# Token scatters of a two-layer gated cross-attention and mixture-of-experts kernel: four in a row per batch, or one by one over two units and over the expert blocks

## The reference, cut to what matters

```python
x = x + tanh(g_xattn[0]) * attention0(layernorm(x), ctx, ctx, mask)
x = x + tanh(g_ffn[0]) * experts0(layernorm(x))     # silu(x@gate[e]) * (x@up[e]) @ down[e], hidden width 688
x = x + tanh(g_xattn[1]) * attention1(layernorm(x), ctx, ctx)
x = x + tanh(g_ffn[1]) * experts1(layernorm(x))     # relu(x@w1[e])**2 @ w2[e], hidden width 256
```

## Time and profile before

| what | value |
|---|---|
| median of three runs | 711.34 us |
| the profiled execution, its span | 741.8 us |
| its own time | the profile gives the span; no other time of that execution is shown |
| PE (TensorE) busy | 659.3 us, 89% |
| DVE (VectorE) busy | 407.1 us, 55% |
| ACT (ScalarE) busy | 271.6 us, 37% |
| POOL (GpSimd) busy | 221.4 us, 30% |
| TensorE clock granted, mean | 0.972 |
| layer 0 units, blocks | 0 to 160 us, 160 to 464 us |
| layer 1 units, blocks | 464 to 612 us, 612 to 722 us |
| last combination and output | 722 to 742 us |

### The profile page before, as it was taken

One profiled execution on the slowest core, in us unless ns is written; L12 is line 12 of the kernel. 1 busy time (PEld: TensorE's weight loads), 2 busy tenths in 40 slices (PEclk: granted clock), 3 DMA queues, 4 the chain that ended last, 5 costly groups with the idle time before them and its releaser, 6 DMA issues.

```text
span 741.8 us, 17801 instructions
## 1 busy us (share of the span) xinstructions
PE 659.3 (89%) x6008; PEld 481.6 (65%) x6008; DVE 407.1 (55%) x1375; ACT 271.6 (37%) x531; POOL 221.4 (30%) x405
## 2 busy tenths in 40 slices
PE   8889887789999999999999999989888888789960
PEld 6657666557777777777775555667666656578730
DVE  3888778774444323332332223688888775554416
ACT  4555555542211111121111112467666432244430
POOL 5123434433231111111111111124655344544430
PEclk9999999999999999999999999999999999899995
DMA  9243434552124111101311100601111132443329
GB/s 231 68 136 124 142 123 169 183 178 67 44 101 120 38 36 29 36 30 36 82 33 41 30 15 18 232 30 31 59 60 59 59 101 86 144 122 115 108 72 339
DMA packets 49960, 69.14 MB, mean 93 GB/s; under 512 B 7751, under 2 KB 37319, under 8 KB 49875
## 3 DMA queue, kind: packets, MB, share of 16 engines
q1 hardware_dynamic: 40620, 49.00, 21.8%
q0 software_dynamic: 6528, 17.90, 6.8%
q10 hardware_dynamic: 2727, 1.11, 0.6%
HBM read 45.76 MB, written 22.23 MB: 92 GB/s over the span
## 4 chain that ended last, share of the span: by engine, by line
PE 70%; DVE 14%; issue 5%; another core or an unknown queue 5%; DMA 2%; ACT 2%; POOL 1%; SPq 0%; ACTq 0%; DVEq 0%; POOLq 0%
PE ps L1764 26%; PE ps L1810 16%; DVE m_rows L981 4%; PE ps L1550 4%; PE ps L1787 3%; PE ps L1488 3%; PE ps L1542 3%; PE ps L1505 2%; PE ps L1588 2%; PE ps L1564 2%; DVE x_sb L965 2%; DVE ctx_q L998 1%; PE ps L1516 1%; DVE share L1003 1%
## 5 line engine op out<-in xcount | busy, mean ns | idle before, releaser
L1764 PE MATMUL ps<-w_all,share 128*128 (+1 forms) x720 | 213.2, 443 | 8.2 <-DVE share L1125 5.8
L1764 PEld LDWEIGHTS ps<-w_all,share 128*128 128x128 f32 (+1 forms) x720 | 125.2, 180 | 73.6 <-issue 13.9
L629 POOL DMA_INDIRECT ys_dram<-share,dest_i x72 | 69.1, 960 | 297.1 <-DVE share L1346 247.5
L1810 PE MATMUL ps<-w_all,share 112*128 (+3 forms) x576 | 139.1, 385 | 5.0 <-ACT share L864 4.3
L1810 PEld LDWEIGHTS ps<-w_all,share 112*128 112x128 f32 (+3 forms) x576 | 98.2, 180 | 24.8 <-issue 8.6
L1405 DVE TENSOR_TENSOR share<-share,ps 128x344 f32<-128x344 f32 x72 | 37.0, 514 | 122.1 <-PE ps L1764 54.1
L981 DVE TENSOR_REDUCE m_rows<-ps 128x8 f32<-128x960 f32 x64 | 70.6, 1143 | 14.4 <-PE ps L1505 9.9
L845 ACT COPY share<-ps 128x512 f32<-128x512 f32 x36 | 21.1, 585 | 141.2 <-PE ps L1787 141.2
L600 POOL DMA_INDIRECT xs_dram<-xn,slot_now x64 | 63.6, 994 | 30.0 <-issue 14.0
L840 ACT ACTIVATE share<-ps 128x344 f32<-128x344 f32 x72 | 32.9, 457 | 96.8 <-PE ps L1764 71.4
L577 POOL TENSOR_SCALAR nm<-mv 128x1 f32<-128x1 f32 (+1 forms) x48 | 11.6, 242 | 157.5 <-DVE mv L1021 120.4
(11 more groups left out here) (235 smaller groups left out, 1102.8 us busy)
## 6 DMA issues: line engine op xcount, KB each, us to landing
w_all<-ys_dram SPq DMA_DIRECT2D x16, 512.0 KB, 7.3
share<-xs_dram SPq DMA_DIRECT2D x56, 129.0 KB
w_all<-gate SPq DMA_DIRECT2D x8, 688.0 KB
w_all<-up SPq DMA_DIRECT2D x8, 688.0 KB
w_all<-down SPq DMA_DIRECT2D x8, 560.0 KB
w_all<-w SPq DMA_DIRECT2D x16, 256.0 KB
share<-xs_dram SPq DMA_DIRECT2D x32, 64.5 KB
out<-x_sb SPq DMA_DIRECT2D x8, 256.0 KB, 5.6
```

Of the source, the lines that this page charges most:

```text
L629: g.indirect_dma_start(ys_dram, bass.IndirectOffsetOnAxis(ap=dest_i[:, u:u + 1], axis=0), y_sb[:, u, :], None).then_inc(D_y[u], 16)
L1764: i = t.matmul(ps[0:r, bank, 0:w], xgT[:, k, 0:r], w_all[:, bass.ds(off + (k * UPW[l] + col - EW[l]), w)], start=(k == 0), stop=(k == KT - 1))
L1810: i = t.matmul(ps[0:n, 6, 0:D], h[:, 0:n], w_all[0:r, bass.ds(off + (KT * UPW[l] + c * D - EW[l]), D)], start=(c == 0), stop=(c == KD[l] - 1))
```

## The change

The scatters get a semaphore for each tile. In an even unit of batch b >= 3 GpSimd now does: the token numbers, scatter (0, 0) of batch b-3, in layer 1 the second addition of batch b+2, a wait for this unit's shifted scores, scatter (0, 1), ln2_rstd of the unit before, ln1_rstd of batch b+2. In the odd unit: scatter (1, 0), in layer 1 the first addition of batch b+3, the same wait, scatter (1, 1), ln2_rstd. After the units the four scatters of batch 5 are placed behind waits for the first up products of blocks 0, 1 and 2 (`up_done`; b_up counts four steps for each of layer 0's blocks and one for each of layer 1's), with the last ln2_rstd and the pad's tile of zeros after the second; then come store 0 and the scatters of batches 6 and 7, each behind block 2 to 9's up products and each ahead of a store. ln2_apply waits for the tile that it overwrites alone; slots and SP wait for both tiles. Nothing is computed differently.

```diff
--- before.py
+++ after.py
@@ -239,7 +239,7 @@
         L_last = sem("last_expert_loaded")
         L_xg = [sem(f"block_loaded{u}") for u in range(U3)]
         D_y = [sem(f"block_stored{u}") for u in range(U3)]
-        D_sc = [sem(f"tokens_scattered{b}") for b in range(NB)]
+        D_sc = [[sem(f"tile{t}_scattered{b}") for t in range(2)] for b in range(NB)]
         D_pad = sem("pads_scattered")
         D_gl = [sem(f"results_loaded{b}") for b in range(NB)]
         D_out = [sem(f"out_stored{i}") for i in range(2)]
@@ -353,9 +353,9 @@
 
             return j // U3 + BLOCKS // U3 * l
 
-        def scattered(B):
-
-            return D_sc[B % NB], 64 * (B // NB + 1)
+        def scattered(B, t):
+
+            return D_sc[B % NB][t], 32 * (B // NB + 1)
 
         UP = [[(0, 0, 344), (1, HID[0], 344), (2, 344, 344), (3, HID[0] + 344, 344)], [(0, 0, HID[1])]]
         REST = (HID[0] - P) // (KD[0] - 1)
@@ -452,7 +452,8 @@
 
                 sp.wait_ge(d_l1, 14 * (l + 1))
                 for b in range(EARLY):
-                    sp.wait_ge(*scattered(NB * l + b))
+                    for t in range(2):
+                        sp.wait_ge(*scattered(NB * l + b, t))
                 sp.wait_ge(p_q, 2 * NB * (l + 1))
                 for j in range(2):
                     load_block(j)
@@ -598,7 +600,7 @@
             def scatter_rows(B, t, k):
                 s = (NU * (B // NB) + 2 * (B % NB)) % 6
                 g.indirect_dma_start(xs_dram, bass.IndirectOffsetOnAxis(ap=slot_now[:, B % 2, t, k:k + 1], axis=0),
-                                     xn2[:, s + t, :], None).then_inc(scattered(B)[0], 16)
+                                     xn2[:, s + t, :], None).then_inc(scattered(B, t)[0], 16)
 
             def token_numbers(B):
                 b = B % NB
@@ -607,12 +609,6 @@
                 g.tensor_copy(xn2[:, s:s + 2, D], tokid[:, 2 * b:2 * b + 2]).then_inc(g_id, 1)
                 g.wait_ge(g_id, B + 1)
                 g.wait_ge(d_slot, B + 1)
-
-            def scatter(B):
-                token_numbers(B)
-                for t in range(2):
-                    for k in range(TOPK):
-                        scatter_rows(B, t, k)
 
             def add_results(b, k):
 
@@ -643,39 +639,58 @@
                     B, G = NB * l + b, NU * l + u
                     if even:
                         if b >= 3:
-                            scatter(B - 3)
-                    elif b + 2 < NB:
-                        ln1_rstd(B + 2)
-                    if u > 0:
+                            token_numbers(B - 3)
+                            scatter_rows(B - 3, 0, 0)
+                        if l == 1 and BY_V <= b + 2 < NB:
+                            add_results(b + 2, 1)
+                        if b >= 3:
+                            g.wait_ge(p_e, G + 1)
+                            scatter_rows(B - 3, 0, 1)
+                        if u > 0:
+                            ln2_rstd(G - 1)
+                        if b + 2 < NB:
+                            ln1_rstd(B + 2)
+                    else:
+                        if b >= 3:
+                            scatter_rows(B - 3, 1, 0)
+                        if l == 1 and BY_V <= b + 3 < NB:
+                            add_results(b + 3, 0)
+                        if b >= 3:
+                            g.wait_ge(p_e, G + 1)
+                            scatter_rows(B - 3, 1, 1)
                         ln2_rstd(G - 1)
-                    if l == 1 and not even and BY_V <= b + 3 < NB:
-                        add_results(b + 3, 0)
-                        add_results(b + 3, 1)
-                scatter(NB * l + NB - 3)
+                B5, B6, B7 = (NB * l + NB - n for n in (3, 2, 1))
+
+                def up_done(j, n):
+
+                    g.wait_ge(b_up, 4 * j + n if l == 0 else 4 * BLOCKS + j + 1)
+
+                token_numbers(B5)
+                scatter_rows(B5, 0, 0)
+                up_done(0, 2)
+                scatter_rows(B5, 0, 1)
                 ln2_rstd(NU * l + NU - 1)
                 for h in range(2):
                     g.wait_ge(p_pv[h], NU * (l + 1))
                 g.memset(zrow, 0.0).then_inc(g_z, 1)
                 g.wait_ge(g_z, 2 * l + 1)
                 g.memset(zrow[:, D:D + 1], 1000000.0).then_inc(g_z, 1)
-                B6, B7 = NB * l + NB - 2, NB * l + NB - 1
+                up_done(1, 1)
+                scatter_rows(B5, 1, 0)
+                up_done(2, 1)
+                scatter_rows(B5, 1, 1)
+                store_block(l, 0)
                 token_numbers(B6)
-                scatter_rows(B6, 0, 0)
-                scatter_rows(B6, 0, 1)
-                store_block(l, 0)
-                scatter_rows(B6, 1, 0)
-                store_block(l, 1)
-                scatter_rows(B6, 1, 1)
-                store_block(l, 2)
-                store_block(l, 3)
+                for n in range(4):
+                    up_done(2 + n, 3)
+                    scatter_rows(B6, n // 2, n % 2)
+                    store_block(l, 1 + n)
                 token_numbers(B7)
-                scatter_rows(B7, 0, 0)
-                store_block(l, 4)
-                scatter_rows(B7, 0, 1)
-                scatter_rows(B7, 1, 0)
-                store_block(l, 5)
-                scatter_rows(B7, 1, 1)
-                for j in range(6, BLOCKS):
+                for n in range(4):
+                    up_done(6 + n, 3)
+                    scatter_rows(B7, n // 2, n % 2)
+                    store_block(l, 5 + n)
+                for j in range(9, BLOCKS):
                     store_block(l, j)
 
 
@@ -751,7 +766,7 @@
                     a.wait_ge(g_rs2, G + 1)
                     need(a, p_x2, G - 5)
                     if G // 2 >= 3:
-                        a.wait_ge(*scattered(G // 2 - 3))
+                        a.wait_ge(*scattered(G // 2 - 3, qt))
                     a.activation(xn2[:, G % 6, 0:D], x_sb[:, G % NU, :], ACT.Identity, bias=nm2[:, qt:qt + 1],
                                  scale=rstd2[:, qt:qt + 1]).then_inc(a_xn2, 1)
 
@@ -1068,7 +1083,8 @@
                     v.tensor_tensor(cumb[:, :], cumb[:, :], maskb[:, 1, :], ALU.add).then_inc(d_cum, 1)
                     v.wait_ge(d_r2, 2 * B + 2)
                     if B >= 2:
-                        v.wait_ge(*scattered(B - 2))
+                        for t in range(2):
+                            v.wait_ge(*scattered(B - 2, t))
                     v.tensor_copy(slot_now[:, B % 2, :, :], slotf[:, :, :]).then_inc(d_slot, 1)
 
                 def route2(B):
```

## The result

Over 14 runs each the changed kernel took 713.07 us (711.99 to 714.97) and the kernel before 711.24 (710.02 to 712.81): ratio 1.0029, 95% interval 1.002 to 1.0037. It is slower by 1.8 us where the forecast had 5.1. But that holds under one of two conditions only. Times taken under different conditions can't be set side by side, so each is given with its "before".

What follows compares the result with a forecast made beforehand. TensorE was taken to bound the kernel, its expert products leading the chain. The terms +4.8 + 4.0 - 2.6 - 1.1 gave +5.1 on 711.34, so 716.4 us; the forecast's own 8-in-10 range was 711 to 721, overall 690 to 721.

Steps and rivals of the forecast that it cites:

- Part 2: Start of the blocks, both layers: batch 4's last scatter now waits for shifted scores, delaying the first load; +4.8 us.
- Part 3: Layer 1's block 13: the last batches' scatters among the blocks make its load late; +4.0 us.
- Part 5: Layer 1's last normalisation: two scatters ahead of it instead of four, ending TensorE's idle wait; -1.1 us.
- Part 4: Layer 1's units 5, 7 and 9: moved additions no longer meet VectorE's divide; -2.6 us.
- part 1: Attention units: scatters spread over two units; normalisations behind the new wait are covered by POOL's wait for VectorE's statistics; 0.
- late signals: Bursts of scatters on POOL: delayed signals totalling 29.7 us, taken to belong mostly to the profiled execution.
- rival (a): Units with four scatters, layer 1's first blocks: burst delays exist unprofiled; 691.2 us (all, chance 0.18) or 703.8 (half, 0.16).

Runs made afterwards that it cites:

- e1: The kernel before, unchanged, run and profiled again: 711.77 us, ratio 1.0001 to before; its profile spans 710.2 us.
- e9: The changed kernel, unchanged, run once more beside the kernel before (711.90 us): 712.75 us, ratio 1.0028.
- e4: The kernel before's units, with the last batches' scatters among the blocks as in the changed kernel: 713.18 us, ratio 1.0024 (before 711.55).
- e17: The kernel before with only the additions moved as in the changed kernel: 714.68 us, ratio 1.0045 (before 711.85).
- e16: The changed kernel with only the additions back at the place they had before: 715.81 us, ratio 1.0067 (before 711.85).
- e8: The changed kernel without the waits of batches 6's and 7's scatters for up products, order kept: 725.36 us, ratio 0.9752 (before 743.29).
- e10: The changed kernel, batch 4's last scatter without its wait, batches 6 and 7 scattered in the order of before: 707.69 us, ratio 0.9949 (before 711.90).
- e15: The changed kernel with the additions and ln1_rstd back behind the odd unit's normalisation: 750.61 us, ratio 1.0077 (before 743.94).
- e11: The changed kernel, unchanged, in a series where the kernel before took 746.00 us: 723.21 us, ratio 0.9700.
- e6: The kernel before with only the additions moved as in the changed kernel: 745.35 us, ratio 1.0028 (before 743.29).

## Why the prediction was wrong, step by step

**The time.** Slower was right, by 1.83 us and not 5.1. The places were right, the start of the blocks and block 13, but most terms of the sum had the wrong size; that the total lay within 3.3 us is partly luck, since the errors were of both signs. Part by part against e1, by the table:

- **Part 2** was 4.8 and is 1.79, the step that failed most by this profile. Two of its terms were too large. From the load's issue to the transposes it is 2.09 and 2.06 us, not 2.99: that row was of a block in two halves, issued one behind the other. And GpSimd's wake behind the shifted scores is 0.3 us, not 0.80. Landing and reading, 2.54 in the sum, took 2.81 and 2.47 us, but 4.0 in layer 1 of e9, so that by e9 the part is 3.1. The Trainium skill's fit (DMA: Bandwidth & Descriptors, Anatomy of one DMA; there measured on DMAs of GpSimd's queue), an estimate of 2.3 for a whole block, was nearer than the row that I let decide. Before's own start in layer 1 varies too: 5.08 in e1, 4.70 in the first profile, in e4 and in e17.
- **Part 3** was 4.0 and is 7.09 (5.0 by e9). The last scatter starts 4.6 us behind block 9's up products, inside my 3.8 to 5.4, and the wait is 4.29. What I left out is that TensorE's clock falls behind such a wait: the two blocks behind it took 2.6 us more than e1's, with groups of matmuls at 1.91 us that take 1.03 otherwise. And before had no stall where I had 0.6.
- **Part 5**: TensorE's idle 1.10 us ahead of the last normalisation's transposes, still there in e1, is gone, as forecast. But blocks 0 to 12 win 3.11 in all, and the other 2 had no term.
- **Part 4** was 2.6 and the units win 3.23. Its mechanism holds on the spread scatters (2.58 from e16 to the changed kernel, as much as the divides lose); it doesn't hold by itself, as e17 shows, and the sum had not seen that it hangs on part 1.
- **The tail's** 1.38 us no part had. Most of it lies in two steps from one block to the next, 2.88 and 3.37 us in e1, 2.16 and 2.83 in the changed kernel; what makes it stays open.

The sum also treated the parts as independent, and they are not. In e1 the last scatter starts at 621.69 and block 13's transposes at 628.35; in the changed kernel at 621.56 and 628.71. TensorE reached block 12 some 4 us sooner (622.09 for 626.19), but GpSimd's queue, full from batch 6's first scatter on (603.12 against 604.71) and with stores 6 and 7 now ahead of the last scatter, kept that scatter at the same time. So the wait for block 13's load swallowed the gain. e8 shows that not the waits for up products do this, e10 that the place does: there the last scatter starts 33.5 us behind layer 1's last shifted scores (583.09 to 616.56), not 36.9, and block 13 doesn't wait.

**The reason under it.** I took the late signals for a product of the profiled execution, since their 29.7 us matched the 30.5 between its span and the median. The match was right and the reading wrong: there is a condition in which unprofiled runs take as long, 743 to 746 us, with the same late signals, and the execution profiled first fits it. e1's profile has none of them at 710.2. What decides the condition isn't known; it lasted for a whole series, and both kinds came on chips with the same number. Where it is present rival (a) holds: it had 691 to 704 on 711, a gain of 7 to 20 us; measured are 22.8 (746.00 to 723.21). Under the other condition there is nothing of this kind to win. The premise that timed runs have nearly no late signals is true of the three runs that it started from and of the result, but it isn't a property of the kernel: with the result taken under the first condition, the forecast would have had the wrong sign.

**The cover of part 1** held: ln2_rstd and the even unit's ln1_rstd behind the new wait cost nothing in layer 0 (65.88 us in e1 and 65.97 in the changed kernel). e15 shows how near the edge it was: with ln1_rstd in the odd unit the same wait goes with 79.8 us where e11 has 68.2. That the change also moves ln1_rstd out of the odd unit I had not priced, and the rest hangs on it.

## What to carry to other kernels

When a profiled execution is far longer than the runs, profile the same kernel again before building on either; a term that exists under one condition only needs a time for each. When the work ahead of a wait gets shorter, look at the queue that ends the wait: here each store more ahead of the last scatter puts it 1.27 us later, and TensorE pays that as waiting and then again as clock. Before trusting a split of the loss by stage, take a second profile. Before putting a wait into a queue, list what stands behind it, and move what the next batch needs ahead.

## What the runs showed of the hardware

The same program ran under two conditions 31 to 35 us apart, neither a matter of the profiler. In one, steps of ScalarE and VectorE that wait for TensorE start up to 6 us late while GpSimd issues indirect DMAs back to back (exp's waits for "remote" of up to 5.9 us in e6, with exp itself unchanged); in the other no profile has such a wait. With two scatters half a unit apart exp has none either (e11), though the units stay 2 to 3 us longer than under the other condition. The cause is open: that it is the signal that comes late is read from the times, since the traces name no releaser.

A wait of TensorE of 4.29 us was followed by a granted clock of 0.62 over 625 to 634 us, that is partly at the lower of its two levels (1.2 of 2.4 GHz): a group of four matmuls took 1.91 us that takes 1.03 otherwise.

In a full queue of GpSimd the indirect DMAs mostly started 1.27 us apart, 0.96 busy and 0.30 between (617.61, 618.88; 620.29, 621.56 in the changed kernel).
